# Context keys of one attention formed a stage earlier, and that attention run two tiles deep

## The reference, cut to what matters

```python
def _L2_attn_ref(hidden_states, Wq, Wk, Wv, Wo):      # 32 heads of 16, 8 key heads, rotary
    q, k, v = hidden @ Wq.T, hidden @ Wk.T, hidden @ Wv.T
    ...                                               # rotary on q and k, causal softmax, @ Wo.T
def _L2_xattn_ref(text, features, Wq, bq, Wk, bk):    # one head of width 512
    Q = jnp.einsum('btx,dx->btd', text, Wq) + bq
    K = jnp.einsum('bpx,dx->bpd', features, Wk) + bk
    scores = jnp.einsum('btd,bpd->btp', Q, K) * scale
    attn = jax.nn.softmax(scores, axis=-1)
    return jnp.einsum('btp,bpd->btd', attn, features)
...
x = x + _L2_attn_ref(_layernorm(x), ...)
x = x + _L2_xattn_ref(_layernorm(x), ctx_4096, ...)
```

## Time and profile before

| | before |
|---|---|
| median of the runs | 4381.8 us |
| profiled execution, its time | 4379.11 us |
| its span | 4377.3 us |
| granted TensorE clock, mean | 0.951 |
| TensorE busy | 4017.6 us, 92% of the span |
| VectorE busy | 2180.6 us, 50% |
| ScalarE busy | 1428.1 us, 33% |
| GpSimd busy | 312.9 us, 7% |

### The profile page before, as it was taken

How to read it: one execution, slowest core, us unless ns; L and a number is a source line. 1 busy time by engine, 2 the same in 40 slices (tenths; PEclk the granted TensorE clock), 3 DMA queues, 4 the chain that set the end, 5 groups by cost and what they waited for, 6 DMA issues and landing times. The chain is left out here.

```text
span 4377.3 us, 52019 instructions
## 1 busy us (share of the span) xinstructions
PE 4017.6 (92%) x19210; PEld 2174.5 (50%) x19210; DVE 2180.6 (50%) x3809; ACT 1428.1 (33%) x2603; POOL 312.9 (7%) x288
## 2 busy tenths in 40 slices
PE   8899989998788999999988779699999899999997
PEld 3334434554355555544446554354555455555654
DVE  0777665553247323224458338766556454444433
ACT  3776754453123211111113234221112132222232
POOL 1011001221001100000000111000000000000000
PEclk9999999999788999999998879899999999999998
DMA  4111121110001423201000122100010011111100
GB/s 176 57 55 35 60 88 39 38 33 31 18 25 59 150 97 117 94 24 69 0 27 1 39 98 54 63 20 20 20 39 20 6 59 34 35 34 39 51 17 22
DMA packets 133915, 215.11 MB, mean 49 GB/s; under 512 B 42704, under 2 KB 95056, under 8 KB 123072
## 3 DMA queue, kind: packets, MB, share of 16 engines
q1 hardware_dynamic: 133696, 212.06, 13.9%
HBM read 167.99 MB, written 44.04 MB: 48 GB/s over the span
## 5 line engine op out<-in xcount | busy, mean ns | idle before, releaser
L810 PE MATMUL l3a_pj<-kvT,l3a_wq 128*128 128x512 f32 x512 | 228.5, 600 | 7.9 <-issue 7.9
L810 PE MATMUL l3x_pj<-kvT,l3x_wq 128*128 128x512 f32 x512 | 229.8, 603 | 3.6 <-issue 3.6
L908 PE MATMUL l3a_po<-l3a_wo,l3a_cT 128*128 128x512 f32 x512 | 230.8, 604 | 2.5 <-ACT l3a_cT L1037 2.2
L432 PE MATMUL l1x_pj<-kvT,l1x_wq 128*128 128x512 f32 x512 | 228.3, 599 | 0.7 <-ACT kvT L240 0.7
L477 PE MATMUL l1x_po<-l1x_wo,l1x_cT 128*128 128x512 f32 x512 | 226.2, 596 | 1.2 <-issue 1.2
L573 DVE TENSOR_TENSOR x<-x,l1x_po 128x512 f32<-128x512 f32 x64 | 44.1, 689 | 267.0 <-PE l1x_po L477 267.0
L810 PEld LDWEIGHTS l3a_pj<-kvT,l3a_wq 128*128 128x128 f32 x512 | 96.7, 192 | 122.1 <-issue 122.0
L810 PEld LDWEIGHTS l3x_pj<-kvT,l3x_wq 128*128 128x128 f32 x512 | 97.1, 193 | 117.9 <-issue 117.9
L908 PEld LDWEIGHTS l3a_po<-l3a_wo,l3a_cT 128*128 128x128 f32 x512 | 95.6, 192 | 120.8 <-issue 111.2
L477 PEld LDWEIGHTS l1x_po<-l1x_wo,l1x_cT 128*128 128x128 f32 x512 | 95.7, 192 | 110.9 <-issue 110.9
L432 PEld LDWEIGHTS l1x_pj<-kvT,l1x_wq 128*128 128x128 f32 x512 | 94.6, 190 | 110.2 <-issue 107.2
(11 more groups left out here) (521 smaller groups left out, 7804.8 us busy)
## 6 DMA issues: line engine op xcount, KB each, us to landing
l1x_kb<-l1x_keys SPq DMA_DIRECT2D x32, 512.0 KB, 4.7
l1x_vb<-l1x_values SPq DMA_DIRECT2D x32, 512.0 KB, 3.3
l1x_keys<-l0a_kv SPq DMA_DIRECT2D x48, 256.0 KB, 2.0
l1x_values<-l0a_kv SPq DMA_DIRECT2D x40, 256.0 KB, 2.3
kvT<-in_L_xattn_Wv SPq DMA_DIRECT2D x8, 1024.0 KB, 5.8
l1x_wq<-in_L_xattn_Wq SPq DMA_DIRECT2D x8, 1024.0 KB, 4.8
l1x_sbias<-in_L_xattn_bias SPq DMA_DIRECT2D x8, 1024.0 KB, 7.3
l1x_wo<-in_L_xattn_Wo SPq DMA_DIRECT2D x8, 1024.0 KB, 5.8
```

The lines of the kernel that those rows point to most:

```text
L432: mm = pe.matmul(pj[:, j, :], wq[:, u, k, h * DH:(h + 1) * DH], m.kvT[:, k, 1, 512 * j:512 * (j + 1)], start=k == 0, stop=k == KC - 1)
L810: mm = pe.matmul(pj[:, j, :], wq[:, u, k, h * DH:(h + 1) * DH], m.kvT[:, k, 1, 512 * j:512 * (j + 1)], start=k == 0, stop=k == KC - 1)
L908: mm = pe.matmul(outs[t % 2][:, :], cT[:, h, t * P:(t + 1) * P], wo[:, u, h, :], start=h == 0, stop=h == GH - 1)
```

## The change

`stage_small_attn` gets a `follower`, given only to the rotary stage. That stage now also loads the full-width stage's key weights into a tile of its own (`next_wk`, `next_bk`) and, behind them, its query weights, query bias and context into tiles that both stages share (`m.next`). Its TensorE does one `unit` per tile: four matmuls of 128x512 that form a quarter of the keys' rows for half of the tokens, into the output's PSUM tile `po`; ScalarE copies it with the bias into `kT2`, which holds the keys of all tokens. ScalarE waits for `next_wk` and `next_bk` before the stage's first norm. Independently of `follower`, both small attentions run the second exponential ahead of the projections' copies.

The full-width stage loses its loads, its key projections and the key biases. Its query projection is cut in two halves with a PSUM tile each; two tiles are normed and turned ahead, the third normed; the probabilities are turned into a PSUM tile of their own (`pp`); VectorE's moments for the next norm stand behind the softmax of a tile and not ahead of it.

```diff
-def stage_l2_xattn(nc, m, ctx_tokens, w_q, b_q, w_k, b_k):
+def stage_l2_xattn(nc, m):
...
-                    for c in range(KC):
-                        for k in range(KC):
-                            mm = pe.matmul(pk[:, c * P:(c + 1) * P], wk[:, k, c * P:(c + 1) * P],
-                                           m.kvT[:, k, 0, n * P:(n + 1) * P], start=k == 0, stop=k == KC - 1)
-                    mm.then_inc(k_ready, 1)
...
-                    pe.wait_ge(q_biased, n + 2)
-                    pe.wait_ge(k_biased, n + 2)
+                    pe.wait_ge(q_biased, 2 * n + 3)
...
+                    if n + 1 < T:
+                        project(n + 1, 0)
+                    if n + 2 < T:
+                        f.turn(pe, n + 2)
                     pe.wait_ge(p_ready, n + 2)
...
+                    pe.transpose(pp[:, 0:P], p[:, :], m.ident[:, :]).then_inc(p_turned, 1)
+                    if n + 1 < T:
+                        project(n + 1, 1)
...
                     nc.scalar.activation(p[:, :], sc[:, :], ACT.Exp, bias=mx[:, :]).then_inc(exped, 1)
+                    if n + 1 < T:
+                        biases(n + 1, 0)
+                    if n + 2 < T:
+                        f.copy(act, n + 2, u)
...
+                    if n + 1 < T:
+                        biases(n + 1, 1)
                     f.out(act, n)
+                    if n + 3 < T:
+                        f.norm(act, n + 3)
...
-def stage_small_attn(nc, m, name, w_q, w_k, w_v, w_o, rope):
+def stage_small_attn(nc, m, name, w_q, w_k, w_v, w_o, rope, follower=None):
...
+                if follower:
+                    sp.dma_start(wk2[:], follower["wk"]).then_inc(next_loaded, 16)
+                    sp.dma_start(bk2[:], follower["bk"]).then_inc(next_loaded, 16)
+                    for key in ("wq", "bq", "ctx"):
+                        sp.dma_start(m.next[key][:], follower[key]).then_inc(given_loaded, 16)
+                    sp.wait_ge(given_loaded, 48)
...
+                def unit(n):
+                    if n == 0:
+                        pe.wait_ge(next_loaded, 32)
+                    pe.wait_ge(f.out_copied, n + 1)
+                    for k in range(KC):
+                        mm = pe.matmul(f.po[:, :], wk2[:, k, (n // 2) * P:(n // 2 + 1) * P],
+                                       m.kvT[:, k, 0, 512 * (n % 2):512 * (n % 2 + 1)], start=k == 0, stop=k == KC - 1)
+                    mm.then_inc(unit_ready, 1)
...
                     turns(n, 0)
                     turns(n, 1)
+                    if follower:
+                        unit(n)
                     if within(n + 1):
                         scores(n + 1, 0)
...
                     exps(n, 0)
                     if within(n + 2):
                         f.norm(act, n + 2)
+                    exps(n, 1)
                     if within(n + 1):
                         copies(n + 1, 1 - u)
-                    exps(n, 1)
...
+                    if follower:
+                        act.wait_ge(unit_ready, n + 2)
+                        nc.scalar.activation(kT2[:, n // 2, 512 * (n % 2):512 * (n % 2 + 1)], f.po[:, :], ACT.Identity,
+                                             bias=bk2[:, n // 2:n // 2 + 1]).then_inc(unit_copied, 1)
...
                 act.wait_ge(zeroed, 2)
+                if follower:
+                    act.wait_ge(next_loaded, 32)
                 f.act(act, 0, 0)
```

More of the change, by code:

```diff
@@ L3216, in stage_l2_xattn @@
         with nc.Block() as block:
[L3217 to L3221, removed]
             @block.gpsimd
@@ L3255, in body @@
                     mm.then_inc(s_ready, 1)
[L3256 to L3259, removed]
+                    if n + 1 < T:
+                        project(n + 1, 0)
+                    if n + 2 < T:
+                        f.turn(pe, n + 2)
                     pe.wait_ge(p_ready, n + 2)
-                    pe.transpose(f.pt[:, 0:P], p[:, :], m.ident[:, :]).then_inc(p_turned, 1)
+                    pe.wait_ge(pT_ready, n + 1)
@@ L3269, in _ @@
+                f.turn(pe, 1)
                 project(0, 0)
+                project(0, 1)
                 every_tile(body)
@@ L3273, in _, with biases @@
             def _(act):
[L3274 to L3282, removed]
+                def biases(n, half):
+                    act.wait_ge(q_ready, 2 * n + half + 2)
+                    act.wait_ge(s_ready, n + 1)
+                    for c in (2 * half, 2 * half + 1):
+                        ins = nc.scalar.activation(qT[:, c, :], pq[half][:, (c % 2) * P:(c % 2 + 1) * P], ACT.Identity,
+                                                   bias=bq[:, c:c + 1])
+                    ins.then_inc(q_biased, 1)
                 def body(n, u):
-                    if not last(n):
-                        f.act(act, n + 1, 1 - u)
                     act.wait_ge(max_ready, n + 2)
                     nc.scalar.activation(p[:, :], sc[:, :], ACT.Exp, bias=mx[:, :]).then_inc(exped, 1)
+                    if n + 1 < T:
+                        biases(n + 1, 0)
+                    if n + 2 < T:
+                        f.copy(act, n + 2, u)
                     act.wait_ge(p_turned, n + 2)
                     act.wait_ge(f.out_ready, n + 1)
-                    nc.scalar.copy(pT[:, :], f.pt[:, 0:P]).then_inc(pT_ready, 1)
-                    if not last(n):
-                        biases(n + 1)
+                    nc.scalar.copy(pT[:, :], pp[:, 0:P]).then_inc(pT_ready, 1)
+                    if n + 1 < T:
+                        biases(n + 1, 1)
                     f.out(act, n)
+                    if n + 3 < T:
+                        f.norm(act, n + 3)
                 f.act(act, 0, 0)
-                act.wait_ge(q_loaded, 32)
-                act.wait_ge(k_loaded, 32)
-                biases(0)
+                f.act(act, 1, 1)
+                f.norm(act, 2)
+                biases(0, 0)
+                biases(0, 1)
                 every_tile(body)
```

63 lines of the change are left out of this document (32 added, 31 removed).

## The result

The changed kernel takes 4317.0 us (median, 4315.5 to 4321.1), the kernel before 4382.7 beside it: ratio 0.9857, interval 0.9842 to 0.9872, 66 us less. Forecast were 4338 and a range of 4328 to 4356: the sign was right, the size was not. The profiled execution took 4315.53 us with a span of 4313.6 (before 4379.11 and 4377.3), so the two profiles compared here lie 63.6 us apart.

What follows compares the result with a forecast made beforehand. TensorE, busy in 92% of the span, was taken as the bound, with VectorE setting the rotary tile. Terms of -42.0, -5.7, +10.2, -8.0 and +1.6 sum to -43.9, giving 4338 us; range 4328 to 4356.

Steps and rivals of the forecast that it cites:

- Term 1: Full-width tiles: period falls from 12.5 to 6.5 us, -42.0 us over seven; bounds -44.1 and -18.2.
- Term 2: Full-width start: loads gone, first scores 9.5 us after the first norm instead of 15.2, -5.7 us.
- Term 3: Rotary start: ScalarE's wait for key weights delays the first norm and projection, +10.2 us.
- Term 4: Rotary tiles: units fill TensorE's gap, exponential's wait goes, period 20.0 us at full clock, -8 us over seven.
- Term 5: Rotary end: the last unit stands between the last turned probabilities and the attention, +1.6 us (0 to +4).
- term 6: Plain small attention: the moved exponential changes nothing, TensorE's output matmuls decide; 0, between -2 and +1 us.
- the kept clock: Rival, rotary tiles: TensorE stays at 0.87 of its clock, period 23.0 us, +13.5 instead of -8, 4359 us; chance 0.13.
- the full-width tile is no chain: Rival, full-width tiles: the tile stays a chain because late probabilities make TensorE stand, +13.3 us, 4351 us; chance 0.08.
- small gaps: Rival, full-width stage: many small gaps lower TensorE's clock to three quarters, period 8.7 us, +15.2 us, 4353; chance 0.05.
- the loads were not shared evenly: Rival, rotary start: further loads share the engines evenly with the key weights, start +18 us, 4346 us; chance 0.03.
- nothing got slower: Rival, rotary stage: bound by TensorE, it falls to a low clock; at 0.6, +86 us, 4429 us; chance 0.03.

Runs made afterwards that it cites:

- the run with the later wait: Changed kernel with ScalarE's wait for the key weights moved from before the rotary stage's first norm to its first unit copy: 4306.8 us, ratio to before 0.9839.
- the kernel before with the move: Kernel before with only the second exponential put ahead of the three copies on ScalarE: 4364.2 us, ratio 0.9962.
- the padded kernels: Satisfied waits added to TensorE's full-width stage: changed kernel plus 45, 75, 121, 377 instructions 4324, 4326, 4341, 4373 us; kernel before plus 135 4378.8 us.
- the kernel before with spread waits: Kernel before with 135 more TensorE instructions, as satisfied waits in four stages ahead of the fourth block where TensorE waits anyway: 4372.0 us, ratio 0.9984.

## Why the prediction was right and wrong

- Term 1, full-width tiles: right in kind, 6.16 us for my 6.5 (-44.3 for -42.0). Output and biases do end together, as I had it, but at 6.1 and not at 6.2 to 6.3, and the 0.15 for waits that I couldn't see was not there. That my lower bound of 6.2 was met is partly luck: I called it TensorE's own work without a wait, but it held 0.3 us of waiting for the probabilities, which scores of 0.99 us for my 0.9 and a turn of 0.54 for 0.4 filled.
- Term 2, start: first scores 9.9 us after the norm for 9.5. Right, with two errors that partly cancel: the queries began at 4.4 us for my 3.6 and took 4.8 for 5.2.
- Term 3, the rotary start: +9.8 for +10.2. Right, and the run with the later wait shows its cause.
- Term 4, rotary tiles: -10.0 for -8, outside my bound of -8.8. Of the two routes, filling TensorE's gap and freeing the exponential, I gave the gain to the first. The runs show that each alone brings 8.0 to 9.5. With both, the five full periods after the first are 19.9 us for my 20.0, and the half-clock stretch for which I allowed 0.8 didn't come. I had read the exponential's wait in one tile, 3.51 us, and not summed it over the tiles: 13.0.
- Term 5, +1.1 for +1.6; term 6, the plain small attention, 172.5 us for 171.3 and 171.3 for 171.3 in the kernel before with the move: nothing beyond what profiles of one order differ by. Right.
- **The step that failed is the sum itself.** "Sum: -42.0 - 5.7 + 10.2 - 8.0 + 1.6" holds the changed stages only; every stage behind stood in it at zero, without a bound. That was worth -17.0. -11.8 of it is the loop of the fourth block's rotary attention, whose two waits at the back-jumps went because code ahead of it was shorter, as the padded kernels show. The trace of before had both waits for anyone who asked for waits put down to "issue". With the changed stages as measured and nothing behind them the forecast would have been 4332.6, inside the range; with the -11.8 alone it would have been 4326, below it.
- The feed-forward stage's -3.7 stays open: it took 254.8 us in the kernel before with spread waits, but 251.2 with 135 more instructions in one place and 251.3 with only the exponential moved, whose code stands where before's does. So the place of TensorE's code doesn't explain it. The thirteen profiles range from 250.6 to 254.8, and TensorE's clock in the stage was 0.87 in before, 0.88 with spread waits and 0.89 in after; what set it is not shown.
- Slips in the sums, without weight here: part 4 bounds the kept clock at +12.8 and the rival at +13.5; the middle of 6.3 and 9.9 is 8.1, not 8.4; 4429 leaves out the 2.7 us that the other sums add (4432).
- The rivals: the clock did not stay at 0.87, the full-width tile is no chain, small gaps don't lower the clock there (1.00), the loads were not shared evenly (+18 forecast, +9.8 seen), nothing got slower.

The Trainium skill, "Runtime: NRT & Kernel Launch", section "Instruction fetch mechanics", says that instructions are fetched in 16 KiB blocks and that a taken branch stalls for a fetch where its target is outside a window of two blocks. The trace agrees with the size (0.49 MB in 30 packets) and with the stall (3.9 us at a back-jump). It does not agree with the window: the section gives two blocks, by which every back-jump of a loop of 1618 instructions would stall, and a buffer of 2048 instructions for TensorE, by which none would; here they do or don't by where the loop begins, and the measurement decides.

## What to carry to other kernels

Ask the trace for waits put down to "issue" at every loop's back-jump, and count the instruction packets inside the loop: a change of length in code far ahead can give or take microseconds a turn (6 here), so an edit's worth is read from its own stages and not from the total alone. A stall that appears in several tiles is summed over them before one tile's figure is used. A wait belongs in front of its first reader, not of the stage: one moved wait was worth as much (10.0 us) as all that the seven rotary tiles gained.

## What the runs showed of the hardware

- The loop of the fourth block's rotary attention costs 0, 1 or 2 fetches for its two back-jumps by the place of its code: 676.1 to 677.1, 682.6 and 686.5 to 689.6 us, in seven, one and five of thirteen kernels. TensorE stands 3.6 to 4.0 us each time, and the slow matmuls behind it (16 in 8.82 us for 7.03) make it about 6.
- 242 satisfied waits on TensorE made their stage 12.9 us longer, 754 made it 40.4 longer: 0.05 us each, not nothing.
- Taking 3.6 us of matmuls out of a tile made it longer by 0.3 us (139.5 for 137.5 us in seven), with TensorE's clock at 0.90 for 0.99. The two periods that kept the full clock took 19.4 us for 19.9.
